# A two-layer GNN over 50,000 nodes: node groups begun ahead, indices copied for three tiles, eight gathers moved across a stage border, a longer ring of edge tiles

## The reference

```
h   = relu(layernorm(x))
# layer 0
msg = relu(h[src] + edge_attr)
t   = h + scatter_add(msg at dst)
t   = batchnorm(t @ W1 + b1) * bn_gamma + bn_beta        # 256 -> 512
t   = relu(t) @ W2 + b2                                  # 512 -> 256
t   = two normalizations over all nodes with ln_*, gn_*  # one graph
x   = x + (h + relu(t))
# layer 1
h   = relu(layernorm(x))
x   = x + relu(h @ W + segment_sum((h @ M)[src], dst))
```

## Time and profile before

| | |
|---|---|
| device time, median of 3 runs | 2557.79 us (2555.56 to 2563.54) |
| the profiled execution's own time | 2563.98 us |
| its span | 2562.2 us |
| share busy over the span | PE 94%, PEld 87%, DVE 84%, ACT 71%, POOL 67% |
| stages 1, 2, 3, 4 | 467, 1205, 595, 295 us |
| mean DMA rate over the span | 208 GB/s |

### The profile page before, as it was taken

The page is one execution under the profiler, slowest core; times in us unless marked ns, Lnnn a source line. Parts: engine busy times, 40 slices in busy tenths (PEclk is TensorE's granted clock), DMA queues, the critical chain, the costliest instruction groups (busy, mean ns, idle before and its releaser), DMA issues. The chain is left out here.

```text
span 2562.2 us, 59007 instructions
## 1 busy us (share of the span) xinstructions
PE 2406.6 (94%) x13809; PEld 2228.8 (87%) x13809; DVE 2144.7 (84%) x6315; ACT 1808.9 (71%) x3908; POOL 1716.1 (67%) x1799
## 2 busy tenths in 40 slices
PE   6899999899999999999999999969999999969897
PEld 5688888699999999999999999958888888858786
DVE  6899999599999999999999999767777777758886
ACT  5799999466666666666666666559888888845554
POOL 5677777466666666666666676347666666737675
PEclk8999999899999999999999999969999999989998
DMA  7999888323444444444444444379999999645553
GB/s 204 243 264 261 261 262 237 93 69 98 156 158 157 156 154 152 152 153 159 159 154 157 152 153 152 113 270 404 381 385 377 374 381 373 242 132 158 157 160 108
DMA packets 310548, 533.61 MB, mean 208 GB/s; under 512 B 74700, under 2 KB 166083, under 8 KB 310454
## 3 DMA queue, kind: packets, MB, share of 16 engines
q1 hardware_dynamic: 250150, 461.89, 53.0%
q0 software_dynamic: 59712, 70.24, 10.3%
q10 hardware_dynamic: 592, 0.54, 0.1%
HBM read 339.38 MB, written 290.19 MB: 246 GB/s over the span
## 5 line engine op out<-in xcount | busy, mean ns | idle before, releaser
L1055 ACT ACTIVATE r<-pair,bnC,bnA 128x384 f32<-128x384 f32 (+1 forms) x524 | 353.2, 674 | 352.7 <-PE pair L1248 352.0
L1008 POOL DMA_INDIRECT ar<-sum_table,idx x391 | 440.3, 1126 | 192.2 <-POOL idx L1004 110.4
L1439 POOL DMA_INDIRECT x1d_table<-x1r,slot x391 | 380.5, 973 | 185.0 <-issue 119.7
L1156 DVE CAST rH<-r 128x384 fp32r<-128x384 f32 (+1 forms) x524 | 393.9, 752 | 43.9 <-ACT r L1055 30.4
L1645 PE MATMUL pair<-Ws,h1T 128*128 128x256 f32 x1564 | 369.4, 386 | 24.0 <-DVE orr L1565 22.1
L1645 PEld LDWEIGHTS pair<-Ws,h1T 128*128 128x128 f32 x1564 | 287.3, 190 | 78.1 <-issue 39.5
L1264 PE MATMUL bank<-rH,W2h 128*128 128x384 f32 x1048 | 352.6, 336 | 1.7 <-ACT yr L1069 1.7
L1264 PE MATMUL bank<-rL,W2h 128*128 128x384 f32 x1048 | 352.4, 336 | 0.0
L1264 PE MATMUL bank<-rH,W2l 128*128 128x384 f32 x1048 | 352.2, 336 | 0.0
L824 PE MATMUL bank<-hr 128*128 128x257 f32 (+1 forms) x1564 | 289.2, 336 | 32.2 <-ACT hr L537 31.7
L1165 DVE TENSOR_TENSOR rL<-r,rH 128x384 fp32r<-128x384 f32 (+1 forms) x524 | 304.0, 580 | 18.0
(11 more groups left out here) (221 smaller groups left out, 5647.9 us busy)
## 6 DMA issues: line engine op xcount, KB each, us to landing
xr<-in_x SPq DMA_DIRECT2D x248, 384.0 KB
x_table<-x1r SPq DMA_DIRECT2D x130, 384.0 KB
out<-orr SPq DMA_DIRECT2D x130, 384.0 KB
xh_table<-xr SPq DMA_DIRECT2D x118, 384.0 KB, 2.3
yT_table<-yr SPq DMA_DIRECT2D x118, 384.0 KB, 2.8
xh_kept<-xh_table SPq DMA_DIRECT2D x86, 384.0 KB, 12.1
y_stays<-yT_table SPq DMA_DIRECT2D x86, 384.0 KB
x1d_table<-blank SPq DMA_DIRECT2D x131, 128.0 KB
```

Of the source, the lines that this page charges most:

```text
L1008: pool.indirect_dma_start(ar[0:p, s, j, :], None, sum_table[:, :], bass.IndirectOffsetOnAxis(ap=idx[0:p, s, j:j + 1], axis=0), bounds_chec ...
L1055: act.activation(r32[:, m, 0:n], z_ps[m][:, 0:n], ACT.Relu, bias=bnC[:, m:m + 1], scale=bnA[:, m:m + 1]).then_inc(r_kept, 1)
L1156: dve.tensor_copy(rH[:, s, m, 0:n], r32[:, m, 0:n]).then_inc(rh_kept, 1)
L1439: pool.indirect_dma_start(x1d_table[:, :], bass.IndirectOffsetOnAxis(ap=slot[0:p, half, s * T + j:s * T + j + 1], axis=0), x1r[0:p, s, j, ...
```

## The change

In stage 1, `AHEAD` becomes 12: eight more groups are begun on every engine before tile 0, and `mixed_rounds` writes out one more of its rounds. VectorE does all index work right after group 0 (group 1 only behind the copies of rows to f32), groups 2 to 7 behind it. SyncE's loads follow that order. GpSimd copies the indices of three tiles at once (`EH` = 3), and waits for their slots' transfers instead of for VectorE; only the first scatter waits for the fill of `id_table`. `ids` is filled and loaded at the end of stage 1. In stage 2 the memset of `blank` moves behind group 1's index copy. At the end of stage 3 GpSimd waits for the writes of `x_table` and gathers the first eight tiles of stage 4 into `W1s` and `W2s`, the weights' f32 tiles, unused by then. In stage 4 the ring has 28 slots instead of 14, and a tile's scatter stands 13 tiles behind its gather instead of 9.

Core of the diff (line shifts, declarations and equal edits for other engines left out):

```diff
+EH = EU // 2
-AHEAD = 4
+AHEAD = 12
...
-    with eng.Fori(2, full - 1) as i:
+    with eng.Fori(2, full - 2) as i:
         one_round(i)
+    one_round(full - 2)
     one_round(full - 1)
...
                 mixed_rounds(sp, group, edge, 0, 8)
                 sp.wait_ge(index_out, 16)
                 sp.wait_ge(ids_clear, 32)
+                sp.wait_ge(ids_set, 1)
+                sp.dma_start(ids[:, 0:TILES], id_table[0:P * TILES, :].rearrange("(p t) a -> p (t a)", t=TILES)
+                             ).then_inc(ids_in, 16)
+                sp.dma_start(ids[0:REST, TILES:TILES + 1], id_table[P * TILES:NODES, :]).then_inc(ids_in, 16)
+                sp.wait_ge(ids_in, 32)
...
-                def set_index(at):
...
-                    after(pool, est_done, t - EU + 1)
-                    after(pool, id_out[s], 16 * used)
+                def set_index(r, half):
+
+                    first = r * EU + half * EH
+                    if is_int(r) and first >= ET:
                         return
...
+                    for s in range(half * EH, half * EH + EH):
+                        after(pool, sd_in[s], 32 * r)
+                        after(pool, id_out[s], 16 * r)
                     pool.nop(nofuse=True)
-                    pool.tensor_copy(idx[:, s, :], index[:, bass.ds(t, 1), :].rearrange("p a b -> p (a b)")
+                    pool.tensor_copy(idx[:, half * EH:half * EH + EH, :], index[:, bass.ds(first, EH), :]
                                      ).then_inc(got_index, 1)
...
-                    set_index(back(at, -1))
+                    if u == EH - 1:
+                        set_index(r, 1)
+                    if u == EU - 1:
+                        set_index(r + 1, 0)
...
+                    if is_int(t) and t == 0:
+                        pool.wait_ge(ids_clear, 32)
...
+                pool.memset(ids[:, TILES:], NO_ROW).then_inc(ids_set, 1)
...
-                pool.memset(ids[:, TILES:], NO_ROW)
-                pool.memset(blank[:], 0.0).then_inc(blank_made, 1)
-                pool.wait_ge(ids_in, 32)
...
+                        if is_int(k) and k == 1:
+                            pool.memset(blank[:], 0.0).then_inc(blank_made, 1)
...
+        EARLY = 8
+
+        def early_rows(t):
+
+            return W1s[:, t // 2, t % 2 * CH:(t % 2 + 1) * CH] if t < 4 else W2s[:, t - 4, :]
...
+                for s in range(RU):
+                    pool.wait_ge(x1_out[s], 16 * (-(-(NG - s) // RU)))
+                pool.nop(nofuse=True)
+                for t in range(EARLY):
+                    pool.indirect_dma_start(early_rows(t), None, x1_table[:, :],
+                                            bass.IndirectOffsetOnAxis(ap=index[:, t, 0:1], axis=0),
+                                            bounds_check=NODES - 1, oob_is_err=False).then_inc(early_in, 16)
+                pool.wait_ge(early_in, 16 * EARLY)
...
-        XU = 14
+        XU = 28
+        LATE = 13
...
-                    if inside(at, ET):
+                    if inside(at, ET) and not is_early(at[0]):
...
-                    late = back(at, 9)
+                    late = back(at, LATE)
```

More of the change, by code:

```diff
@@ L395, in _ @@
                 sp.dma_start(id_table[P * TILES:NODES, :], no_rows[0:REST, 0:1]).then_inc(ids_clear, 16)
+                for k in range(1, 4):
+                    group((k, k, 0, GU))
                 sp.wait_ge(flag_made, 1)
@@ L409, in _ @@
                 sp.dma_start(dst_table.rearrange("(t p) -> t p", p=P), dst_rows[:]).then_inc(dst_out, 16)
+                for k in range(4, GU):
+                    group((k, k, 0, GU))
+                sp.dma_start(W1s[:], W1.rearrange("(k p) n -> p k n", p=P)).then_inc(split_loaded, 16)
+                sp.dma_start(W2s[:], W2.rearrange("(k p) n -> p k n", p=P)).then_inc(split_loaded, 16)
                 sp.wait_ge(dst_out, 16)
@@ L412, in _ @@
                 sp.dma_start(index_table[:, :, :], index[:]).then_inc(index_out, 16)
+                for k in range(GU, AHEAD):
+                    group((k, k % GU, k // GU, GU))
                 mixed_rounds(sp, group, edge, 0, 8)
@@ L586, in _ @@
                 for k in range(AHEAD):
-                    group((k, k, 0, GU))
+                    group((k, k % GU, k // GU, GU))
                 row = 0
@@ L766, in _ @@
                 dve.tensor_copy(rows_f[:, 2, :], next_rows[:]).then_inc(rows_float, 1)
-                group((2, 2, 0, GU))
+                group((1, 1, 0, GU))
                 dve.wait_ge(turned, 1)
@@ L800, in _ @@
                                          op0=ALU.mult, op1=ALU.mult).then_inc(index_made, 1)
-                group((3, 3, 0, GU))
+                for k in range(2, GU):
+                    group((k, k, 0, GU))
                 dve.wait_ge(split_loaded, 32)
@@ L979, in step @@
                     if inside(at, NG):
+                        if is_int(at[0]) and at[0] == 0:
+                            sp.wait_ge(blank_made, 1)
                         sp.dma_start(x1d_table[bass.ds(at[0] * P, P), :], blank[:]).then_inc(slots_clear, 16)
@@ L1700, in gnn_kernel, with source_rows, is_early @@
             enb = sb("f_nb", [P, XU, 2], scope=scope)
+            def source_rows(s):
+                return early_rows(s) if s < EARLY else e_s[:, s - EARLY, :]
+            def is_early(t):
+                return is_int(t) and t < EARLY
             sT_ps = [bank[i][:, 0:CH] for i in range(2)]
@@ L1806, in step @@
                         dve.wait_ge(d4_in[s], 16 * (used + 1))
-                        dve.wait_ge(s4_in[s], 16 * (used + 1))
-                        dve.bn_stats(est6[:, s, 0, :], e_s[:, s, :])
+                        if not is_early(t):
+                            dve.wait_ge(s4_in[s], 16 * (used if s < EARLY else used + 1))
+                        dve.bn_stats(est6[:, s, 0, :], source_rows(s))
                         dve.bn_stats(est6[:, s, 1, :], e_d[:, s, :]).then_inc(st4_done, 1)
```

35 lines of the change are left out of this document (13 added, 22 removed).

## The result

The changed kernel takes 2541.05 us (median of 4 runs, 2540.17 to 2542.31) against 2560.35 us of the kernel before in the same session; the ratio is 0.992, with a 95% interval of 0.9902 to 0.9937. The profiled execution has a span of 2540.7 us, 21.5 less than before.

What follows compares the result with a forecast made beforehand. Stage 1 was held by TensorE, VectorE and ScalarE together, stage 4 by GpSimd's indirect DMAs. Stage 4 -17.6, two seams +0.5 each and stage 1 -3 made -19.6 on the profiled execution, so 2538 us for the median; range 2524 to 2549.

Steps and rivals of the forecast that it cites:

- (a): Whole kernel: the forecast itself comes true, 2530 to 2547 us; chance 0.62.
- Eight gathers leave GpSimd's queue, 8 x 1.32 = 10.6: Stage 4: eight gathers fewer on GpSimd's queue save 10.6 us if nothing else limits.
- "cover" of 18 us instead of 7.5: Stage 4: slack between a tile's result and its scatter, 18 us with lag thirteen, 7.5 with nine, to absorb stalls.
- GpSimd ends a block with a DRAIN, 10.99 us here; it would ... end at 2266.5: Stage 3's end: DRAIN starts at 2255.5 after the early gathers, just using up the flush's cover until about 2266; +0.5 us.
- tile 0 +11: Stage 1's start: eight more groups ahead put VectorE's tile 0 at 38 us against 27.20, +11.
- Filling, copies and the shorter last round: Stage 1, tiles 0 to 90: filling buffers during groups -8, fewer index copies -3, seven groups in the last round -1.3.
- The tail from tile 90 to 98: Stage 1's end: GpSimd's 3.75 us a tile sets the pace, 23.5 us against 27.3, -3.8.
- Index work first ... Two us, costed at nothing: Stage 1's start: earlier index work saves two us, counted as nothing since tile 0 waits for VectorE's turn.
- (e): Stage 1: TensorE at half clock through the groups ahead, 22 us, eats the gain, 2560 us; chance 0.06.
- (d): Stage 1: three-tile copies wait for landings, 2.5 us 32 times, 80 us slower, 2618 us; chance 0.03.
- (c): Stage 4 gives only 8 to 10 us, stage 1 loses 3 to 6, 2548 to 2556 us; chance 0.16.
- (b): Stage 1 gives 13 us for filling, 6 for copies, stage 4 up to 21, 2519 to 2530 us; chance 0.13.

Runs made afterwards that it cites:

- early0: Changed kernel without the eight early gathers, ring of 28 and lag of 13 kept; 2538.05 us (one run).
- stage1_part: Kernel before with only the edits of stage 1 and its seam with stage 2; 2920.39 us where the kernel before took 2916.24, ratio 1.0015.
- direct: Changed kernel with the indices of stage 4's first 28 tiles taken from SBUF and a lag of 18; 2536.7 us, ratio to before 0.9913.
- ahead4: Changed kernel with four groups ahead of tile 0 instead of twelve; 2532.51 us (one run).
- tile_copies: Changed kernel with one index copy for each tile instead of one for three; 2902.8 us (one run) where the kernel before took 2917.71.
- fill_behind: Changed kernel with the fill of id_table issued behind the loads of groups 1 to 3; 2536.39 us, ratio to before 0.9917.

## Why the prediction was right, point by point
**The sum.** 2538 forecast, 2541.05 measured; -19.6 forecast for the profiled execution, -21.5 measured. Forecast (a) is the case that came. That the sum is so near is in part luck: stage 1 gave 2.6 us and stage 4's end 2.2 us more than forecast, and stages 2 and 3, beyond the seam's +1.1, took 2.7 back, within their spread.

**Stage 4.** The forecast was -17.6 for the last scatter. Measured from the stage's start it went from 284.2 to 266.8, so -17.4. Counted from 2265.8, where the stage began before, the first scatter was forecast at 24.9 us (2290.7) and gather 98 at 248.0 (2513.8); they came at 25.3 and 248.6. Not forecast: from the last scatter's issue to the end it took 10.0 us instead of 12.2.
The path (GpSimd's queue from the index of tile 13 on) was right, and the timeline worked out along it came true. But the step "Eight gathers leave GpSimd's queue, 8 x 1.32 = 10.6" named the wrong cause: early0 keeps the eight gathers on the queue and its last scatter goes out only 1.1 us later. That the same 10.6 fits is luck. Gather 98 went from 265.4 to 248.6 us after the stage's start, 16.8 earlier, and the rows divide this so: 14 tiles are gathered ahead of the first scatter instead of ten, during a wait that exists anyway, and four tiles of 2.64 us are 10.6; the first scatter is 3.2 us later, at 25.3 instead of 22.1; and the five waits of GpSimd that are gone come to 8.8. That makes 16.2 of the 16.8.
The first part comes from the lag, the last from VectorE's waits at the jumps, which the ring of 28 has not. Among the runs beside 2558 us none had one without the other. That the ring and the lag together carry stage 4's gain is shown by early0; the division between them is read from the trace and not tested.
The rule of the Trainium skill ("Runtime: NRT & Kernel Launch", "Instruction fetch mechanics"), that a taken branch beyond the held pages waits for a fetch, fits with where the waits stand; that a fetch is what VectorE waits for is in no row. Nor does any row say why stage1_part, with the same loop, went without the waits. The "cover" of 18 us instead of 7.5 was argued and not shown.

**The seam of stages 3 and 4.** +0.5 forecast, 0 measured. The step "GpSimd ends a block with a DRAIN, 10.99 us here; it would ... end at 2266.5" failed: behind gathers whose landing had been waited for it took 2.26 us, and in early0, without them, 10.75. The cover was not used up, 8.4 us of it are left.

**The seam of stages 1 and 2.** +0.5 forecast. From SyncE's block end to TensorE's first product of stage 2 it took 25.6 us instead of 24.5: +1.1.

**Stage 1.** -3 forecast, -5.6 measured (-4.3 in early0 and direct). By the terms: tile 0 +11 forecast, +11.9 measured. Two errors cancel in it: TensorE's first group product began at 22.94 instead of 18.6, and from then on a group took it 2.0 us instead of 2.23.
Filling, copies and the shorter last round were forecast at -12.3 between tiles 0 and 90; it was -16.6. Set against ahead4, the eight groups gave back 5.2 us between tiles 0 and 18, 1.3 up to tile 84 and 0.8 in the last round. The tail from tile 90 to 98 was forecast at 23.5 us and took 26.7 (27.3 before): -0.6 instead of -3.8, for tile 98 still waits for its gather. In all, eight groups ahead cost 0.6 us at SyncE's block end, against 1.7 by 11 - 8 - 1.3.
What gives the gain is the rest of the change: ahead4, with four groups as before, has stage 1 at 457.0, 6.2 us less. Its rounds between tiles 24 and 84 take 253.6 us against 255.7, 0.21 us each, or 3.1 for fifteen. These rounds differ in GpSimd's part alone, the copies of three tiles and what they wait for; 3 was forecast. It rests on one profile of each kernel, and the only run that undid the copies (tile_copies) decides nothing.
(By the rule of the Trainium skill in "SBUF — State Buffer", "Who interferes with whom", it would have been 13 if every copy met a two-port operation of VectorE; these rounds don't show that.)
More of the gain stands elsewhere: the first three rounds took 83.9 us against 89.3, with the weights' loads and the fill in another order, and tiles 84 to 90, the round that `mixed_rounds` now writes out, took 23.6 against 25.3. Which edit did either was not separated.
The step "Index work first ... Two us, costed at nothing" had the time wrong: the index was ready at 19.8 us instead of 15.7, for VectorE stood 5.3 us for a load that the fill of `id_table`, now ahead of it, had slowed. Its reason held all the same. Tile 0 waits for VectorE's turn: in fill_behind group 1 came 4.5 us earlier and tile 0 only 1.3.

**The rivals.** (e) did not come: the clock over 20 to 100 us was granted at 0.96, against 0.85 before. It was at the lower level (0.50) up to 26 us, and TensorE's first group took 4.1 us, but it was full from 30 us on, when two of the twelve groups were done. (d) did not: a round is shorter. (c) began 7 us above the measured time, (b) ended 11 us below it.

## What to carry to other kernels
When a queue bounds a stage, count its instructions only from the moment it can run: work taken off it is worth nothing if its first wait is for something else. Here SyncE's index loads held it until 15.9 us into the stage, in plain sight in the profile of after, and taking eight gathers off it gained 1.7 us at most. A wait called "issue" at the places where a loop jumps back is worth a try with fewer passes; here it went with them, though one kernel with the same loop had none. And undo the parts of a bundle one by one: of those undone here the ring and the lag together carried stage 4's gain, and the early gathers and the twelve groups next to nothing; what carried stage 1's is known for about half of it, and not by a run of its own.

## What the runs showed of the hardware
- Behind a DMA that fills 200 KB of DRAM from SBUF, 3072-byte read packets took 1.27 us instead of 0.13 for some microseconds; in two orders of the loads, whichever stood behind it were hit.
- GpSimd's DRAIN at a block's end took 10.99 us behind scatters just issued (10.75 in early0) and 2.26 us behind eight gathers that had landed.
- VectorE stood 2.5 to 4.0 us at each of four jumps back of a 14-tile loop in the kernel before, and at most 0.3 us under "issue" ahead of the same line in stage1_part, whose loop is the same.
- In stage 4 before, TensorE's granted clock was 0.62 around such a wait (2382 to 2391 us), and 0.96 over 2296 to 2530; without the waits it was 1.00 over 2290 to 2530.
- The same kernel took 2558 or 2916 us by the chip or its load, with 374 or 284 GB/s in stage 3, and there the half of the change that lies in stage 1 gave nothing that could be measured.
